# Low parts of the last three units on one engine, and own tiles for the last residual rows

## The chip, the core and the metric

The kernel runs on one core of a Trainium2 chip. The metric is the time of one execution on the device in microseconds (us). TensorE (PE) multiplies matrices, VectorE (DVE), ScalarE (ACT) and GpSimd (POOL) work elementwise, SyncE (SP) issues most of the transfers (DMA). Each engine runs its own instructions in program order, and they wait for each other through semaphores.

## What is computed

A block of two parts on `x` of 2 x 2048 rows of 512 numbers. With `ln` for a normalisation of rows:

```python
x = x + tanh(g_xattn) * xattn(ln(x), ctx, mask)   # 16 heads of 32, 128 keys for each batch
x = x + tanh(g_ffn) * ffn(ln(x))                  # residual inside: h + 0.5 * (silu(LN(h) @ w1 + b1) @ w2 + b2)
# xattn: q = LN(x) @ w_q; k, v = LN(ctx) @ w_kv; softmax(q k^T * scale + mask) v @ w_proj + b_proj
# w1 (512 x 2048), w2 (2048 x 512): (integers - 128) * scales
```

## The kernel before

**Precision.** Most products are made from split operands: a tile is kept as a high part and a low part (what the rounding left over), and `split_product` adds three matmuls (high*high, high*low, low*high; lines 219 to 221). So each operand costs an elementwise subtraction for its low part somewhere.

**Attention** (`attention`, the first 437 us). The 4096 rows are 8 chunks of 512 rows; a chunk is 4 units, each with one group of 4 heads (`HG`), so there are 32 units (`UNITS`), 0 to 31. Every engine walks through steps: step k works on unit k and, beside it, on neighbours: the queries of unit k+2, the maxima of unit k+1, the softmax of unit k, the weighted values of unit k-1, the projection of the row tile k-5, the residual sum of tile k-6. A row tile is 128 rows; 4 of them belong to a chunk. The first and the last steps are written out, the ones between run in a hardware loop; the order in each engine is the order in its `step` function.

**Probabilities.** For each of the four heads j, PE makes the scores into a bank `ps_s` (L522), ACT writes `p_f` (f32, L686) and `p_hi` (f16, L688) from it, and the low part `p_lo = p_f - p_hi` is made by DVE for j = 0 and 1 (L833) and by POOL for j = 2 and 3 (L1006). `weighted_values` (L537, then L541 for the sums of the probabilities) needs all eight parts and runs one step later, behind the maxima matmuls (L504) of the unit after. Its 28 matmuls run in groups of four, one for each head, so 12 + 8 + 8 of them stand in the rows. On DVE a step is: two maxima (L796), the residual sum `x_out = projection + x_res` (L841), two maxima, the inversion of the sums, `p_lo` 0 and 1, `normalise` (L825, `o_f`). The third maxima matmul waits for the first maximum (its bank), the fourth for the second.

**Residual rows.** For tile t, SP loads 128 rows of `x` into `x_res[t % 2]` in step t+4 (L408). That load waits until the residual sums up to tile t-2 are made (L841), as that frees the buffer. POOL adds the bias in step t+5 (`bias_residual`, L983), DVE makes the sum in step t+6, SP stores it (L415). At the end PE projects tiles 28 and 29 in step 33 and 30 and 31 in step 35, by turns into two banks (`ps_xp` for even tiles, `ps_qm` for odd ones); the projection of 31 needs the bank of 29, so it waits for the sum of tile 29.

**The change-over.** The weights of the second part are loaded into memory that attention has given up: `load_w2` is issued by ACT in step 32 (two transfers of 1 MB) after waits on the counts of `p_lo`. DVE and ACT make the first parts of w1 in steps 33 and 35 (L171, L160, L175). Then all engines leave attention together and start `feed_forward`: PE with L219 on `ps_y`, whose sums (`ps_z`, L1228 to L1230) wait for parts of w2 from DVE (L177).

**Memory.** `xt_f`, two tiles of 2 KB a partition, hold a transposed block of normalised x for its splitting. Attention uses them last for job 35, whose low part POOL makes in step 29. `xt_hi` and `xt_lo` are four tiles of 8 KB a partition; small tiles (statistics, scales, maxima) lie behind them.

Of the kernel before, what the change touches and what calls it, by code (L numbers as in the profile page):

```python
# [27 lines left out]
F32R = mybir.dt.float32r  # L28
# [3 lines left out]
ALU = mybir.AluOpType  # L32
# [3 lines left out]
P = 128  # L36
HEAD = 32
HG = P // HEAD
# [11 lines left out]
def build(nc, x, ctx, mask, g_xattn, g_ffn, w_q, w_kv, w_proj, b_proj, g_x, b_x, g_kv, b_kv,  # L50
# [22 lines left out]
    with ExitStack() as whole:  # L73
        def sb(name, shape, dt, scope=whole):
            return scope.enter_context(nc.sbuf_tensor(name, shape, dt))
# [14 lines left out]

        x_in, x_norm = sb("x_in", [P, TT, D], F32), sb("x_norm", [P, TT, D], F32)
        xt_f = [sb(f"xt_f{n}", [P, CHUNK], F32) for n in range(2)]
        xt_hi = [sb(f"xt_hi{n}", [P, KB, CHUNK], F32R) for n in range(2)]
        xt_lo = [sb(f"xt_lo{n}", [P, KB, CHUNK], F32R) for n in range(2)]
        stats, mean_var = sb("x_stats", [P, TT, 6], F32), sb("x_mean_var", [P, TT, 2], F32)
        ln_a, ln_r1, ln_b, ln_c, ln_r2, ln_s2, ln_r, u_scale = (
            sb(n, [P, TT], F32) for n in ("ln_a", "ln_r1", "ln_b", "ln_c", "ln_r2", "ln_s2", "ln_r", "u_scale"))
# [1 line left out]
        fill_col = sb("fill_col", [P, B], F32)  # L99
        ones16 = sb("ones16", [P, HEAD], BF16)  # L100
        maxima = [sb(f"maxima{n}", [P, TT, HG], F32) for n in range(2)]

# [120 lines left out]
def attention(nc, env):  # L225
# [30 lines left out]
    with ExitStack() as scope:  # L256
# [68 lines left out]
             "setup_over"))  # L325
        x_loaded = sem("x_loaded")
        res_loaded = [sem("res_loaded0"), sem("res_loaded1")]
        q_stored, q_packed, max_packed = ([sem(f"{name}{n}") for n in range(2)] for name in ("q_stored", "q_packed", "max_packed"))
        (stats_some, stats_ready, ln_step, rstd_ready, norm_ready, xt_turned, xt_f_ready, xt_hi_ready, xt_lo_ready,
         q_done, q_hi_ready, q_lo_ready, max_done, max_taken, max_turned, max_row_ready, s_done,  # L330
# [33 lines left out]
        def load_vectors(eng, which):  # L364
            for n in which:
                v, at = vectors[n], n * KB
                eng.dma_start(vec_rows[at:at + v.shape[0] // P, :], v.rearrange("(n p) -> n p", p=P)).then_inc(vec_loaded, 16)

        def proj_bank(i, k):

            return ps_qm if not real(i, k + KB, UNITS) and k % 2 else ps_xp
# [7 lines left out]
        def _(sp):  # L379
# [12 lines left out]
            def step(i, k):  # L392
                if real(i, k + 1, UNITS):
                    pack_queries(i, k + 1)
                if k == FIRST:
                    load_x(i, 0)
                if k % KB == 2:
                    load_x(i, k // KB + 3)
                tile = k - 4
                if isinstance(i, int) and PER * i + tile == 0:  # L400
                    sp.wait_ge(wq_lo_ready, 2)
                    sp.wait_ge(wp_lo_ready, 2)
                if real(i, tile, UNITS):
                    c, t = tile // KB, tile % KB
                    source = x_tiles[c % 2, i + c // 2, t, :, :]
                    sp.lower_val(source.offset * 4)
                    after(sp, x1_ready, PER * i + tile - 1)
                    sp.dma_start(x_res[t % 2][:, :], source).then_inc(res_loaded[t % 2], 16)  # L408
                tile = k - 6
                if real(i, tile, UNITS):  # L410
                    c, t = tile // KB, tile % KB
                    target = x1_tiles[c % 2, i + c // 2, t, :, :]
                    sp.lower_val(target.offset * 4)
                    after(sp, x1_ready, PER * i + tile + 1)
                    sp.dma_start(target, x1_out[t % 2][:, :]).then_inc(x1_stored[t % 2], 16)  # L415
                if real(i, k + 2, UNITS):
                    store_queries(i, k + 2)
                if real(i, k + 1, UNITS):
                    pack_maxima(i, k + 1)
# [62 lines left out]
        def _(pe):  # L482
# [42 lines left out]
            def weighted_values(i, k):  # L525


                v, b, m = PER * i + k, (k // KB) % 2, k % KB
                after(pe, p_hi_ready, HG * (v + 1))
                after(pe, p_lo_dve, HG // 2 * (v + 1))  # L530
                after(pe, p_lo_pool, HG // 2 * (v + 1))
                after(pe, o_f_ready, v)
                terms = [(v_parts[0], p_hi), (v_parts[1], p_hi), (v_parts[2], p_hi), (v_parts[0], p_lo), (v_parts[1], p_lo)]
                for n, (part, probs) in enumerate(terms):
                    for j in range(HG):
                        h = HG * m + j
                        nc.tensor.matmul(ps_o[HEAD * j:HEAD * (j + 1), :], part[:, b, h * HEAD:(h + 1) * HEAD], probs[j][:, :],  # L537
                                         start=(n == 0), stop=(n == len(terms) - 1))
                for n, probs in enumerate((p_hi, p_lo)):
                    for j in range(HG):  # L540
                        last = nc.tensor.matmul(ps_den[HEAD * j:HEAD * (j + 1), :], ones16[:, :], probs[j][:, :],  # L541
                                                start=(n == 0), stop=(n == 1))
                last.then_inc(pv_done, 1)
# [126 lines left out]
        def _(act):  # L670
# [6 lines left out]
            def probabilities(i, k, j):  # L677

                v, b = PER * i + k, (k // KB) % 2
                if isinstance(i, int) and v == 0 and j == 0:  # L680
                    act.wait_ge(fill_ready, 1)
                    act.wait_ge(setup_over, 2)
                after(act, s_done, HG * v + j + 1)

                after(act, p_lo_dve if j < HG // 2 else p_lo_pool, HG // 2 * (v - 1) + j % (HG // 2) + 1)
                nc.scalar.activation(p_f[j][:, :], ps_s[j % 2][:, :], ACT.Exp, bias=fill_col[:, b:b + 1]).then_inc(p_f_ready, 1)  # L686
                after(act, pv_done, v)
                nc.scalar.activation(p_hi[j][:, :], ps_s[j % 2][:, :], ACT.Exp, bias=fill_col[:, b:b + 1]).then_inc(p_hi_ready, 1)  # L688
# [84 lines left out]
            def last_steps(u):  # L773

                if u == UNITS - 2:
                    act.wait_ge(q_done, UNITS)
                    g("load_w1")(act, 0)
                if u == UNITS:
                    act.wait_ge(s_done, HG * UNITS)
                    act.wait_ge(p_lo_dve, HG // 2 * UNITS)  # L780
                    act.wait_ge(p_lo_pool, HG // 2 * UNITS)
                    g("load_w2")(act, 0)
                if u in (UNITS + 1, UNITS + 3):
                    g("weights_hi")(act, 0, (u - UNITS) // 2)
# [5 lines left out]
        def _(dve):  # L790
# [44 lines left out]
            def add_residual(i, k):  # L835
                tile = PER * i + k
                after(dve, proj_done, tile + 1)
                after(dve, res_biased, tile + 1)
                if real(i, k - 2, UNITS):
                    after(dve, x1_stored[k % 2], 8 * (tile - k % 2))  # L840
                nc.vector.tensor_tensor(x1_out[k % 2][:, :], proj_bank(i, k)[:, :], x_res[k % 2][:, :], ALU.add).then_inc(x1_ready, 1)  # L841

            def row_stats(i, c):
                if not real(i, KB * c, UNITS + KB):
# [23 lines left out]
            def step(i, k):  # L868
                if real(i, k + 1, UNITS):
                    take_max(i, k + 1, (0, 1))  # L870
                if real(i, k - 6, UNITS):
                    add_residual(i, k - 6)
                if real(i, k + 1, UNITS):
                    take_max(i, k + 1, (2, 3))
                if real(i, k + 2, UNITS):
                    queries_lo(i, k + 2)
                if k % KB == 0 and k != -KB:
                    row_stats(i, k // KB + 2)
                if k % KB == 1:
                    normalise_rows(i, k // KB + 2)  # L880
                if real(i, k - 1, UNITS):
                    invert_sums(i, k - 1)
                if real(i, k, UNITS):
                    probabilities_lo(i, k, 0)
                    probabilities_lo(i, k, 1)
                if real(i, k - 1, UNITS):
                    normalise(i, k - 1)
                if isinstance(i, int):
                    last_steps(PER * i + k)

# [88 lines left out]
        def _(pool):  # L979
            def bias_residual(i, k):  # L980
                tile = PER * i + k
                after(pool, res_loaded[k % 2], 8 * (tile - k % 2) + 16)
                nc.gpsimd.tensor_tensor(x_res[k % 2][:, :], x_res[k % 2][:, :], bp_rows[:, :], ALU.add).then_inc(res_biased, 1)  # L983

            def outputs_lo(i, k):
                v, c, m = PER * i + k, (k // KB) % 2, k % KB
# [48 lines left out]
            def step(i, k):  # L1035
                if real(i, k + AHEAD, UNITS + KB):
                    x_lo(i, k + AHEAD)
                if real(i, k - 5, UNITS):
                    bias_residual(i, k - 5)
                if k % KB == 0 and k != -KB:  # L1040
                    row_scales(i, k // KB + 2)
                if real(i, k, UNITS):
                    probabilities_lo(i, k, 2)
                    probabilities_lo(i, k, 3)
                if real(i, k - 1, UNITS):
                    outputs_lo(i, k - 1)
# [363 lines left out]
```

## Time and profile before

| what | us |
|---|---|
| median of 3 runs | 1169.83 |
| lowest and highest of them | 1168.03, 1169.94 |
| the profiled execution | 1169.56 |
| its span in the profile | 1167.7 |
| PE busy | 1102.7 |
| DVE, ACT, POOL busy | 631.1, 389.9, 343.0 |

The span runs from the first to the last instruction of the profile; the execution's own time is 1.86 us longer. "Idle before" in square brackets is how long the engine stood still before an instruction, and after the arrow who released it. `x4` behind a row says that four instructions are merged in it. `ps_z<-w_hi,y_hi` reads "writes ps_z, reads w_hi and y_hi"; buffer numbers are left out.

### The profile page before, as it was taken

How to read it: one execution, taken by the hardware profiler on the slowest of the kernel's cores; microseconds unless marked ns; L12 is line 12 of the kernel's file. 1: busy time of each engine (PE TensorE's matmuls, PEld its weight loads, DVE VectorE, ACT ScalarE, POOL GpSimd, SP SyncE). 2: the span in 40 equal slices, each digit the busy share in tenths (PEclk: the TensorE clock that was granted, in tenths of full speed). 3: DMA queues.
4: the chain of work that ended last, by engine and by line, in shares of the span. 5: the costliest groups of instructions: out<-in, count | busy, mean ns of one | idle time of the engine just before them, and what ended most of it. 6: DMA issues, size and time to landing. Idle time of an engine off the chain costs nothing.

```text
span 1167.7 us, 15594 instructions
## 1 busy us (share of the span) xinstructions
PE 1102.7 (94%) x5433; PEld 845.6 (72%) x5433; DVE 631.1 (54%) x1039; ACT 389.9 (33%) x614; POOL 343.0 (29%) x344
## 2 busy tenths in 40 slices
PE   5778999999989878999999999999999999999998
PEld 3455667666666547888888888888888888888887
DVE  5667788787796647765334335335235235235212
ACT  3467667667667623331121121121111111111110
POOL 4545576676675542202101102102102102012000
PEclk9879999999999989999999999999999999999999
DMA  7665666666655659501002001001000100200000
GB/s 257 154 190 139 180 190 189 203 181 186 210 154 164 186 175 314 155 1 73 1 1 72 1 1 48 25 1 39 33 0 30 42 0 1 72 1 1 37 1 36
DMA packets 61178, 109.20 MB, mean 94 GB/s; under 512 B 9368, under 2 KB 10560, under 8 KB 60608
## 3 DMA queue, kind: packets, MB, share of 16 engines
q1 hardware_dynamic: 58632, 104.11, 29.2%
q10 hardware_dynamic: 2488, 4.34, 1.2%
q8 instruction: 34, 0.56, 0.2%
q14 instruction: 24, 0.20, 0.1%
HBM read 72.51 MB, written 33.55 MB: 91 GB/s over the span
## 4 chain that ended last, share of the span: by engine, by line
PE 61%; DVE 1%; issue 0%; ACT 0%; DVEq 0%
PE ps_y L221 10%; PE ps_y L220 10%; PE ps_z L1228 10%; PE ps_z L1230 10%; PE ps_z L1229 10%; PE ps_y L219 10%; PE ps_h L1242 1%; DVE x_in L1348 0%; DVE x L1311 0%; DVE y_hi L1288 0%; DVE w_lo L177 0%; DVE w_f L171 0%; ACT w_hi L162 0%; DVE y_lo L1290 0%; DVEq L47 0%
## 5 line engine op out<-in xcount | busy, mean ns | idle before, releaser
L1288 DVE CAST y_hi<-y_f 128x512 fp32r<-128x512 f32 x128 | 63.3, 494 | 391.5 <-ACT y_f L1263 391.5
L1263 ACT ACTIVATE y_f<-ps_y,cols 128x512 f32<-128x512 f32 x128 | 88.1, 689 | 552.7 <-PE ps_y L221 552.7
L1228 PE MATMUL ps_z<-w_hi,y_hi 128*128 128x512 f32 x512 | 203.1, 397 | 3.0 <-DVE w_lo L177 3.0
L219 PE MATMUL ps_y<-xt_hi,w_hi 128*128 128x512 f32 x512 | 202.1, 395 | 1.5 <-PEq L256 1.5
L221 PE MATMUL ps_y<-xt_hi,w_lo 128*128 128x512 f32 x512 | 203.4, 397 | 0.0
L220 PE MATMUL ps_y<-xt_lo,w_hi 128*128 128x512 f32 x512 | 202.9, 396 | 0.0
L1230 PE MATMUL ps_z<-w_hi,y_lo 128*128 128x512 f32 x512 | 200.8, 392 | 0.0
L1229 PE MATMUL ps_z<-w_lo,y_hi 128*128 128x512 f32 x512 | 200.4, 391 | 0.0
L219 PEld LDWEIGHTS ps_y<-xt_hi,w_hi 128*128 128x128 f32 x512 | 96.3, 188 | 24.7 <-issue 1.9
L1228 PEld LDWEIGHTS ps_z<-w_hi,y_hi 128*128 128x128 f32 x512 | 96.5, 188 | 23.8 <-DVE w_lo L177 3.4
L220 PEld LDWEIGHTS ps_y<-xt_lo,w_hi 128*128 128x128 f32 x512 | 96.7, 189 | 22.8
L221 PEld LDWEIGHTS ps_y<-xt_hi,w_lo 128*128 128x128 f32 x512 | 96.2, 188 | 22.5
L1230 PEld LDWEIGHTS ps_z<-w_hi,y_lo 128*128 128x128 f32 x512 | 96.4, 188 | 21.1
L1229 PEld LDWEIGHTS ps_z<-w_lo,y_hi 128*128 128x128 f32 x512 | 96.6, 189 | 20.8
L1290 DVE TENSOR_TENSOR y_lo<-y_f,y_hi 128x512 fp32r<-128x512 f32 x128 | 96.4, 753 | 4.4
L1006 POOL TENSOR_TENSOR p_lo<-p_f,p_hi 128x512 f16<-128x512 f32 x64 | 78.9, 1243 | 63.9 <-ACT p_hi L688 63.5
L796 DVE TENSOR_REDUCE maxima<-ps_max 128x4 f32<-128x512 f32 x128 | 81.9, 680 | 13.4 <-PE ps_max L504 13.2
L686 ACT ACTIVATE p_f<-ps_s,fill_col 128x512 f32<-128x512 f32 x128 | 86.3, 674 | 5.1 <-PE ps_s L522 5.1
L688 ACT ACTIVATE p_hi<-ps_s,fill_col 128x512 f16<-128x512 f32 x128 | 85.4, 667 | 0.0
L1366 POOL TENSOR_TENSOR ln_a<-x_mean_var,eps 128x4 f32<-128x4 f32 x7 | 1.5, 216 | 273.0 <-DVE x_mean_var L1333 273.0
L997 POOL TENSOR_TENSOR xt_lo<-xt_f,xt_hi 128x512 fp32r<-128x512 f32 x36 | 46.7, 1300 | 85.6 <-ACT xt_f L698 82.8
L1384 POOL TENSOR_TENSOR x<-x,b_rows 128x512 f32<-128x512 f32 x16 | 26.3, 1672 | 153.3 <-DVE x L1348 153.3
(161 smaller groups left out, 1615.3 us busy)
## 6 DMA issues: line engine op xcount, KB each, us to landing
q_pack<-q_dram SPq DMA_DIRECT2D x96, 256.0 KB, 3.9
x_in<-in_x SPq DMA_DIRECT2D x8, 1024.0 KB, 7.5
q_dram<-q_hi SPq DMA_DIRECT2D x32, 256.0 KB, 2.9
q_dram<-q_lo SPq DMA_DIRECT2D x32, 256.0 KB, 3.3
x_res<-in_x SPq DMA_DIRECT2D x32, 256.0 KB, 3.9
x_dram<-x_out SPq DMA_DIRECT2D x32, 256.0 KB, 4.2
q_raw<-in_L_ffn_fc_q SPq DMA_DIRECT2D x6, 1024.0 KB, 18.6
s_raw<-in_L_ffn_fc_scales SPq DMA_DIRECT2D x6, 1024.0 KB, 17.1
```

The source lines that it names most:

```text
L219: nc.tensor.matmul(out, s_hi, m_hi, start=(k == 0), stop=False)
L220: nc.tensor.matmul(out, s_hi, m_lo, start=False, stop=False)
L221: last = nc.tensor.matmul(out, s_lo, m_hi, start=False, stop=(k == n - 1))
L686: nc.scalar.activation(p_f[j][:, :], ps_s[j % 2][:, :], ACT.Exp, bias=fill_col[:, b:b + 1]).then_inc(p_f_ready, 1)
L688: nc.scalar.activation(p_hi[j][:, :], ps_s[j % 2][:, :], ACT.Exp, bias=fill_col[:, b:b + 1]).then_inc(p_hi_ready, 1)
L796: nc.vector.reduce_max(maxima[k % 2][:, t, :], ps_max[t % 2][:, :].rearrange("p (j n) -> p j n", j=HG), AX.X).then_inc(max_taken, 1)
L1006: nc.gpsimd.tensor_tensor(p_lo[j][:, :], p_f[j][:, :], p_hi[j][:, :], ALU.subtract).then_inc(p_lo_pool, 1)
L1228: nc.tensor.matmul(ps_z[t][:, :], hi, w2_hi[:, f, :], start=(f == 0), stop=False)
L1229: nc.tensor.matmul(ps_z[t][:, :], hi, w2_lo[:, f, :], start=False, stop=False)
L1230: last = nc.tensor.matmul(ps_z[t][:, :], lo, w2_hi[:, f, :], start=False, stop=(f == FB - 1))
L1263: nc.scalar.activation(y_f[f % 2][:, :], ps_y[f % 2][:, :], ACT.Silu, bias=b1_c[:, f:f + 1]).then_inc(y_f_ready, 1)
L1290: nc.vector.tensor_tensor(y_lo[f % 4][:, :], y_f[f % 2][:, :], y_hi[f % 4][:, :].bitcast(F32), ALU.subtract).then_inc(y_lo_ready, 1)
```

## The change

Three things. In units 29, 30 and 31 DVE makes the low parts of heads 2 and 3 too, after `normalise` and ahead of the next step; POOL makes none there. The counts that PE and ACT wait for are adapted (`lo_counts`, `lo_taken`). The residual rows of tiles 30 and 31 go into `xt_f[0]` and `xt_f[1]`; SP loads both in step 30, once the low part of job 35 is made, in place of the loads in steps 34 and 35. And `xt_hi`, `xt_lo` are allocated behind the small tiles, which so move down by four times 8 KB.

```diff
@@ build
-        xt_hi = [sb(f"xt_hi{n}", [P, KB, CHUNK], F32R) for n in range(2)]
-        xt_lo = [sb(f"xt_lo{n}", [P, KB, CHUNK], F32R) for n in range(2)]
         stats, mean_var = sb("x_stats", [P, TT, 6], F32), sb("x_mean_var", [P, TT, 2], F32)
...
         maxima = [sb(f"maxima{n}", [P, TT, HG], F32) for n in range(2)]
+        xt_hi = [sb(f"xt_hi{n}", [P, KB, CHUNK], F32R) for n in range(2)]
+        xt_lo = [sb(f"xt_lo{n}", [P, KB, CHUNK], F32R) for n in range(2)]
@@ attention
+        last_res_loaded = [sem(f"last_res_loaded{n}") for n in range(2)]
+        def in_tail(i, k):
+            return isinstance(i, int) and PER * i + k >= UNITS - 3
+        def lo_counts(i, k):
+            v = PER * i + k
+            more = max(0, v + 1 - (UNITS - 3)) if isinstance(i, int) else 0
+            return HG // 2 * (v + 1 + more), HG // 2 * (v + 1 - more)
+        def lo_taken(i, k, j):
+            v = PER * i + k
+            if in_tail(i, k):
+                return p_lo_dve, lo_counts(i, k - 1)[0] + j + 1
+            return p_lo_dve if j < HG // 2 else p_lo_pool, HG // 2 * v + j % (HG // 2) + 1
+        def last_pair(i, k):
+            return isinstance(i, int) and PER * i + k >= UNITS - 2
+        def residual(i, k):
+            return xt_f[k % 2][:, :] if last_pair(i, k) else x_res[k % 2][:, :]
@@ SP, step
-                if real(i, tile, UNITS):
+                if real(i, k, UNITS) and PER * i + k == UNITS - 2:
+                    sp.wait_ge(xt_lo_ready, UNITS + KB)
+                    for n in range(2):
+                        sp.dma_start(xt_f[n][:, :], x_tiles[(NCHUNK - 1) % 2, (NCHUNK - 1) // 2, KB - 2 + n, :, :]
+                                     ).then_inc(last_res_loaded[n], 16)
+                if real(i, tile, UNITS) and not last_pair(i, tile):
@@ PE, weighted_values
-                after(pe, p_lo_dve, HG // 2 * (v + 1))
-                after(pe, p_lo_pool, HG // 2 * (v + 1))
+                after(pe, p_lo_dve, lo_counts(i, k)[0])
+                after(pe, p_lo_pool, lo_counts(i, k)[1])
@@ ACT, probabilities
-                after(act, p_lo_dve if j < HG // 2 else p_lo_pool, HG // 2 * (v - 1) + j % (HG // 2) + 1)
+                after(act, *lo_taken(i, k - 1, j))
@@ ACT, last_steps
-                    act.wait_ge(p_lo_dve, HG // 2 * UNITS)
-                    act.wait_ge(p_lo_pool, HG // 2 * UNITS)
+                    act.wait_ge(p_lo_dve, lo_counts(0, UNITS - 1)[0])
+                    act.wait_ge(p_lo_pool, lo_counts(0, UNITS - 1)[1])
@@ DVE, add_residual
-                nc.vector.tensor_tensor(x1_out[k % 2][:, :], proj_bank(i, k)[:, :], x_res[k % 2][:, :], ALU.add).then_inc(x1_ready, 1)
+                nc.vector.tensor_tensor(x1_out[k % 2][:, :], proj_bank(i, k)[:, :], residual(i, k), ALU.add).then_inc(x1_ready, 1)
@@ DVE, step
                 if real(i, k - 1, UNITS):
                     normalise(i, k - 1)
+                if real(i, k, UNITS) and in_tail(i, k):
+                    probabilities_lo(i, k, 2)
+                    probabilities_lo(i, k, 3)
@@ POOL, bias_residual
-                after(pool, res_loaded[k % 2], 8 * (tile - k % 2) + 16)
-                nc.gpsimd.tensor_tensor(x_res[k % 2][:, :], x_res[k % 2][:, :], bp_rows[:, :], ALU.add).then_inc(res_biased, 1)
+                if last_pair(i, k):
+                    pool.wait_ge(last_res_loaded[k % 2], 16)
+                else:
+                    after(pool, res_loaded[k % 2], 8 * (tile - k % 2) + 16)
+                nc.gpsimd.tensor_tensor(residual(i, k), residual(i, k), bp_rows[:, :], ALU.add).then_inc(res_biased, 1)
@@ POOL, step
-                if real(i, k, UNITS):
+                if real(i, k, UNITS) and not in_tail(i, k):
                     probabilities_lo(i, k, 2)
                     probabilities_lo(i, k, 3)
```

## Rows read from the trace of the kernel before

**Rows 1.** The page: span and the first line of part 1.
```profile
span 1167.7 us, 15594 instructions
...
PE 1102.7 (94%) x5433; PEld 845.6 (72%) x5433; DVE 631.1 (54%) x1039; ACT 389.9 (33%) x614; POOL 343.0 (29%) x344
```

**Rows 2.** Windows: busy PE, PEld, DVE, ACT, POOL, then clock, DMA share, GB/s.
```profile
300.00:400.00 100.00, 93.14 (x597) 63.17 (x595) 77.45 (x125) 68.01 (x116) 60.62 (x54) 0.98 0.60 172
400.00:420.00 20.00, 13.91 (x86) 7.90 (x87) 8.48 (x14) 7.10 (x13) 10.43 (x10) 0.83 0.55 164
420.00:440.00 20.00, 15.34 (x60) 11.88 (x59) 10.81 (x11) 3.58 (x4) 8.83 (x7) 0.91 0.68 228
```

**Rows 3.** Waits of PE, 380 to 470 us: us in total, times, longest.
```profile
PE ps_o L537 <- POOL p_lo L1006: 6.4, 3, 2.9
PE ps_qm L219 <- DVE x_out L841: 3.1, 1, 3.1
...
PE ps_z L1228 <- DVE w_lo L177: 3.0, 1, 3.0
```

**Rows 4.** Timeline at unit 29: start, duration, instruction, idle before.
```profile
389.47 0.69 DVE L833 TENSOR_TENSOR p_lo<-p_f,p_hi 128x512 f16<-128x512 f32 x1 [0.45 <-ACT p_hi L688]
...
390.08 0.68 DVE L825 TENSOR_TENSOR o_f<-ps_o,inv_den 128x512 f32<-128x512 f32 x1
...
390.66 2.35 POOL L1006 TENSOR_TENSOR p_lo<-p_f,p_hi 128x512 f16<-128x512 f32 x2 [2.18 <-ACT p_hi L688]
390.74 1.29 DVE L796 TENSOR_REDUCE maxima<-ps_max 128x4 f32<-128x512 f32 x2
391.03 0.68 ACT L688 ACTIVATE p_hi<-ps_s,fill_col 128x512 f16<-128x512 f32 x1
...
391.58 1.01 PE L504 MATMUL ps_max<-k_hi,q_hi 128*128 128x512 f32 x2 [0.72 <-DVE maxima L796]
...
391.95 0.68 DVE L841 TENSOR_TENSOR x_out<-ps_xp,x_res 128x512 f32<-128x512 f32 x1
...
393.26 0.83 PE L537 MATMUL ps_o<-p_hi,v 128*32 128x512 f16 x12 [0.67 <-POOL p_lo L1006]
```

**Rows 5.** Timeline at units 30 and 31.
```profile
399.67 2.34 POOL L1006 TENSOR_TENSOR p_lo<-p_f,p_hi 128x512 f16<-128x512 f32 x2 [4.20 <-ACT p_hi L688]
...
400.04 0.68 ACT L688 ACTIVATE p_hi<-ps_s,fill_col 128x512 f16<-128x512 f32 x1
...
402.26 1.47 PE L537 MATMUL ps_o<-p_hi,v 128*32 128x512 f16 x12 [2.85 <-POOL p_lo L1006]
...
412.23 1.46 PE L537 MATMUL ps_o<-p_hi,v 128*32 128x512 f16 x12 [2.85 <-POOL p_lo L1006]
```

**Rows 6.** Timeline of PE: two waits of 1.7 us in earlier units.
```profile
215.11 1.09 PE L504 MATMUL ps_max<-k_hi,q_hi 128*128 128x512 f32 x2 [1.73 <-DVE maxima L796]
...
349.10 1.00 PE L504 MATMUL ps_max<-k_hi,q_hi 128*128 128x512 f32 x2 [1.70 <-DVE maxima L796]
...
350.86 0.63 PE L220 MATMUL ps_qm<-xt_lo,wq_hi 128*128 128x512 f32 x1
```

**Rows 7.** Timeline of the last tiles.
```profile
418.54 0.69 DVE L841 TENSOR_TENSOR x_out<-ps_xp,x_res 128x512 f32<-128x512 f32 x1 [0.52 <-PE ps_xp L221]
...
419.26 0.33 SPq L408 DMA_DIRECT2D x_res<-in_x  x1
...
427.42 2.48 POOL L983 TENSOR_TENSOR x_res<-x_res,bp_rows 128x512 f32<-128x512 f32 x2 [5.16 <-DMA x_res<-in_x]
...
428.77 0.69 DVE L841 TENSOR_TENSOR x_out<-ps_qm,x_res 128x512 f32<-128x512 f32 x1 [4.20 <-POOL x_res L983]
...
435.52 0.69 DVE L841 TENSOR_TENSOR x_out<-ps_qm,x_res 128x512 f32<-128x512 f32 x1 [0.67 <-PE ps_qm L221]
...
437.02 0.47 PE L219 MATMUL ps_y<-xt_hi,w_hi 128*128 128x512 f32 x1 [1.54 <-PEq L256]
```

**Rows 8.** The bias sums, ns: least, median, most.
```profile
L983 POOL TENSOR_TENSOR x_res<-x_res,bp_rows x7: 1262/1270/2278, 394.2 to 432.5; 128x512 f32<-128x512 f32 x7
```

## The prediction

> **What bounds the kernel now.** I read the page first: PE is busy for 94% of the span, so a change elsewhere counts only where PE stands still or its clock is down [rows 1]. The windows show where that is near the change. From 300 to 400 us PE is busy for 93% at a granted clock of 0.98; from 400 to 420 us for 70% at 0.83, from 420 to 440 us for 77% at 0.91 [rows 2]. The list of waits says on what: 6.4 us in three waits for the low parts on POOL, 3.1 us once for a residual sum, 3.0 us once for a part of w2, which comes behind the change-over [rows 3]. The first is what the moved low parts aim at, the second is where the residual tiles would have to act. The timelines say what is behind each.
>
> **The low parts, units 30 and 31.** In unit 30 ACT finishes the last `p_hi` at 400.04 + 0.68 = 400.72, POOL has both low parts at 399.67 + 2.34 = 402.01, and PE starts at 402.26, 0.25 later [rows 5]. On DVE the third low part can be made while ACT works on the fourth head. The fourth starts when `p_hi` is there, plus the hand-over from engine to engine: the first of the two bias sums ends at 427.42 + 1.24 = 428.66 and DVE starts at 428.77, so 0.11 [rows 7]. It takes 0.69 [rows 4]. That is 400.72 + 0.11 + 0.69 = 401.52, against 402.01: 0.5 us earlier. Unit 31 has the same wait of 2.85 [rows 5], so 0.5 us again. Nothing that PE wants soon stands behind them on DVE there: there are no more maxima, and the residual sum that moves behind them feeds a projection that PE reaches after its weighted values. Gain 1.0 us; bounds: 0, if the hand-over to PE is longer from DVE, and 1.2.
>
> **The low parts, unit 29.** Here the maxima of unit 31 stand behind them. Before, DVE goes from `o_f` at 390.08 straight into two maxima at 390.74 (1.29, so 0.645 each), and PE's third maxima matmul starts 0.2 after the first of them, at 391.58 [rows 4]. Now DVE waits for the last `p_hi` (391.03 + 0.68 = 391.71), has the fourth low part at 391.71 + 0.11 + 0.69 = 392.51 and the first maximum at 393.15. PE's third maxima matmul starts at 393.35 and, with the pair's 1.01 kept, the weighted values at about 394.2 to 394.4, where they start at 393.26 now [rows 4]. So this unit loses 0.9 to 1.1 us, of which the wait of 0.67 for POOL is already taken off. I take 1.0. It is on PE's path: the turned maxima come behind the weighted values in PE's order, and the second pair of maxima is late by as much. Queued on DVE behind the same wait are the residual sum of tile 24 (0.68) and two more maxima; that sum delays two transfers on SP, which has a step of room for them.
>
> **The sum of the low parts** is +1.0 - 0.5 - 0.5 = 0.0 us. ACT loses nothing: its waits on the low parts are for those of the unit before.
>
> **The residual tiles.** PE's 3.1 us is the projection of tile 31, which waits for the sum of tile 29 (428.77). That sum waits 4.20 for the bias sum, and this one 5.16 for its load [rows 7]. That is the load of tile 29, issued at 419.26, as soon as the sum of tile 27 (418.54) has freed the buffer [rows 7]. Tile 29 is not one of the two that get tiles of their own, and its buffer is still freed by tile 27. So PE's wait stays. What changes is behind it: the loads of 30 and 31 are early, and the bias sum of 31 follows that of 30 at once. But the sum of tile 31 waits 0.67 for PE, not for its residual [rows 7]. Gain 0; lower bound 0, upper bound 3.1, if the load of 29 came early by other means. SP issues two transfers (0.33 each, by the same kind [rows 7]) in step 30 in place of two later ones. Its new wait is for work of step 29, so it is over; behind it are a load, a store and the packing of the maxima of unit 31, wanted a step later. Cost 0, and 0.7 if that room were not there.
>
> **POOL beside DVE.** The bias sums take 1.27 in the median and 2.28 in one case [rows 8], so a neighbour can hold one up. With the bias sum of 31 moved forward it falls on DVE's second part of w1. If DVE stands still for it, that is 1.27, of which the wait of 0.67 covers half [rows 7]; the other 0.6 is the upper bound. I take 0, as the sum of tile 30 between them waits for its projection as well. The Trainium skill ("SBUF — State Buffer", the section on SBUF's two separate sides) has it that VectorE with two SBUF inputs and GpSimd reading SBUF exclude each other for a whole instruction. It speaks against putting more two-input work on DVE beside POOL, and by it the full 1.27 would be paid on DVE; the longest row above fits it.
>
> **The memory.** Small tiles and `xt_hi`, `xt_lo` change addresses and no instruction changes shape. No row shows a duration that depends on an address. Cost 0; bounds 0.3 either way, the agreement that rows of one kind show (1262 and 1270 ns, the least and the median [rows 8], so under 1% of what touches the tiles).
>
> **The clock.** The 12 matmuls behind the waits of 2.85 take 1.47 and those at 393.26 take 0.83 [rows 4, 5]: the clock is at 1.2 instead of 2.4 GHz there. For 28 matmuls that is 28/12 x 0.64 = 1.5 us, the price of one fall. The waits of 2.85 become 2.35, and a new idle stretch appears in step 30: from 390.86 (391.58 less the 0.72 idle) to 393.35, 2.5 us, where the clock does not fall now. Is 2.35 or 2.5 enough? A stretch of 1.73 at 215 us was not; one of 1.70 at 349 us was, the matmul at 350.86 takes 0.63 [rows 6]; both of 2.85 were. So more likely than not for each of the three, and not certain for any. The likeliest number of falls stays at two. [...]
>
> **Forecast.** 0.0 us from low parts, residuals and memory, with two falls as before. The profiled execution took 1169.56 (span 1167.7), 0.3 below the median of the runs. The forecast of no change goes onto the median: 1169.8. Chance 0.45.
>
> **Rival 1: a third fall** in step 30, none saved: +1.5, 1171.3. For it: the new stretch of 2.5 us. Against it: the 1.73 at 215 us. Chance 0.27. It is slower, but under the bound below.
>
> **Rival 2: the shorter waits save the clock** in one or both of units 30 and 31: -1.5, 1168.3, or -3.0, 1166.8. Chance 0.14, of that 0.04 for both.
>
> **Rival 3: tile 29 is helped after all**, as its load no longer shares the queues with later ones: the 3.1 us go, and the fall of the clock behind them: up to -4.6, 1165.2. Against it: at 419.26 the loads of 30 and 31 were not issued yet. Chance 0.05.
>
> **Rival 4: slower.** The place is the maxima of unit 31 on DVE. The loss of 1.0 is there and the clock falls (1.5); it decides if the low parts of units 30 and 31 give back nothing, because PE's start there is then set by the delayed chain of maxima, their packing and the scores: +2.5, 1172.3. Against it: packing has a step of room. Chance 0.07. That addresses matter, or that the change does not do what it says, has 0.02.
>
> **Range and chances.** A measurement can tell 0.2%, 2.3 us, from no change. The forecast, rival 1 and single savings lie inside. Faster: both savings (0.04), rival 3 (0.05) and the scatter of the runs, which reach 1.8 below their median (0.03): 0.12. Slower: rival 4 (0.07) and the scatter on top of rival 1 with half of the rest (0.04): 0.11. Same: 0.77. The range from 1167.6 to 1171.8 holds the forecast, rival 1 and rival 2 with one saving.
>
> **What would show it.** In the profile after: weighted values of unit 29 about 1 us later (start near 394.3), those of 30 near 402.8, of 31 near 412.2, each behind DVE's low parts instead of POOL's; an idle stretch of 2.5 us before the maxima matmul; the wait of about 3 us for the sum of tile 29 unchanged, with the load of 29 landing some 8 us after its issue; PE's start on `ps_y` within 0.5 us of 437.0 but for the clock, whose share from 390 to 420 us tells the number of falls. I am wrong if that start is over 2.3 us away, or if the wait for the sum of tile 29 is gone.

## The result and the profile after

| | kernel before | changed kernel |
|---|---|---|
| median of 3 runs, us | 1169.83 | 1152.72 |
| lowest and highest, us | 1168.03, 1169.94 | 1151.14, 1154.12 |
| ratio, 95% interval | | 0.9858 [0.9833, 0.9883] |
| span of the profiled execution, us | 1167.7 | 1150.9 |

The changed kernel is 17 us faster. I had forecast no change, 1167.6 to 1171.8 us. Measured once more, beside 11 runs of the kernel before, it gained 12.5 us (changed_again below), so a few of the 17 us are scatter of the runs. The page of the changed kernel, the lines that answer to [rows 1]:

```profile
span 1150.9 us, 15594 instructions
...
PE 1082.7 (94%) x5433; PEld 841.0 (73%) x5433; DVE 634.4 (55%) x1045; ACT 390.1 (34%) x614; POOL 337.1 (29%) x338
```

PE is busy for 20 us less with the same 5433 matmuls, and its share of the span is still 94%. It did not wait less; its matmuls got shorter. Six elementwise instructions went from POOL to DVE, as the diff says.

**Where the time went.** I cut the span at two marks that both timelines have. The first is the `normalise` of unit 28, the last DVE instruction ahead of the new low parts; the second is PE's first matmul on `ps_y`, the start of the second part. The timeline of the changed kernel, DVE and then PE, has

```profile
386.28 0.68 DVE L856 TENSOR_TENSOR o_f<-ps_o,inv_den 128x512 f32<-128x512 f32 x1
...
432.83 0.47 PE L219 MATMUL ps_y<-xt_hi,w_hi 128*128 128x512 f32 x1 [1.54 <-PEq L256]
```

and the kernel before has these marks at 390.08 and 437.02 [rows 4, 7].

| stretch | before, us | after, us | difference |
|---|---|---|---|
| start to the first mark | 390.08 | 386.28 | -3.8 |
| first to second mark (low parts, residual tiles) | 46.94 | 46.55 | -0.4 |
| second mark to the end | 730.7 | 718.1 | -12.6 |

The stretch that I had worked through row by row moved by 0.4 us. Three quarters of the gain is in the second part, in which no instruction was changed. The groups of PE from 700 to 1000 us show it, first for the kernel before (count | busy us, mean ns | idle):

```profile
L1228 PE MATMUL ps_z<-w_hi,y_hi 128*128 128x512 f32 x214 | 84.7, 396 | 0.0
L221 PE MATMUL ps_y<-xt_hi,w_lo 128*128 128x512 f32 x212 | 84.2, 397 | 0.0
L220 PE MATMUL ps_y<-xt_lo,w_hi 128*128 128x512 f32 x212 | 84.0, 396 | 0.0
L219 PE MATMUL ps_y<-xt_hi,w_hi 128*128 128x512 f32 x212 | 83.6, 394 | 0.0
L1229 PE MATMUL ps_z<-w_lo,y_hi 128*128 128x512 f32 x214 | 83.5, 390 | 0.0
```

and for the changed one:

```profile
L1265 PE MATMUL ps_z<-w_hi,y_hi 128*128 128x512 f32 x216 | 85.2, 394 | 0.0
L221 PE MATMUL ps_y<-xt_hi,w_lo 128*128 128x512 f32 x218 | 84.8, 389 | 0.0
L219 PE MATMUL ps_y<-xt_hi,w_hi 128*128 128x512 f32 x217 | 84.4, 389 | 0.0
L220 PE MATMUL ps_y<-xt_lo,w_hi 128*128 128x512 f32 x217 | 84.4, 389 | 0.0
L1267 PE MATMUL ps_z<-w_hi,y_lo 128*128 128x512 f32 x216 | 84.1, 390 | 0.0
```

In the same 300 us, 212 matmuls of each line on `ps_y` became 217 or 218. The matmuls are back to back, without idle time, at full clock. All have one shape. Yet before, those that write `ps_y` took 394 to 397 ns and one that writes `ps_z` 390; after, those on `ps_y` took 389. The `ps_z` row with `w_hi,y_hi` fits neither: it is the longest on `ps_z` before (396) and after (394). As durations overlap, start to start is the better measure. Medians by position in the group of twelve that a step makes, worked out from the start times behind 500 us (a sum is good to 3 ns, as some medians waver between 226 and 227):

```
ps_y before   234 232 231 232 238 237 231 234 235 233 232 237   sum 2806 ns
ps_y after    227 227 227 227 226 227 227 227 227 227 227 227   sum 2723 ns
ps_z before   231 232 231 227 226 227 227 227 227 227 227 227   sum 2736 ns
ps_z after    227 226 227 227 227 227 227 226 227 227 226 227   sum 2721 ns
```

That is 98 ns a step, and 128 steps make 12.5 us, nearly all of the second part's gain. The first three matmuls on `ps_z` were slow before too (231, 232, 231), though neither of their tiles moved; they stand right behind the matmuls on `ps_y`. How the pace reaches over to them is not shown. `ps_y` reads `xt_hi` and `xt_lo` as moving tiles, the ones whose place in memory the change moves; the weights stay where they were.

**Before the second part.** The queries of attention read the same tiles, in 384 matmuls. Start to start on `ps_qm` they take 233 ns before and 227 after in the median, 233.7 and 229.1 in the mean, so they make 1.8 to 2.3 us of the 3.8. The rest fits the clock, granted at 0.84 from 60 to 100 us before and at 0.91 after, and at 0.66 from 350 to 355 us before and at 1.00 after. The first window of the changed kernel, then the second of the kernel before:

```profile
60.00:100.00 40.00, 30.20 (x187) 18.73 (x186) 27.97 (x50) 28.54 (x49) 18.27 (x20) 0.91 0.60 173
```

```profile
350.00:355.00 5.00, 5.00 (x39) 2.73 (x37) 2.03 (x4) 2.04 (x3) 1.02 (x2) 0.66 0.51 179
```

**The stretch of the forecast.** The windows that answer to [rows 2]:

```profile
400.00:420.00 20.00, 16.68 (x105) 11.59 (x106) 13.05 (x19) 7.13 (x11) 8.50 (x6) 0.91 0.75 236
420.00:440.00 20.00, 15.28 (x60) 11.92 (x59) 12.17 (x12) 3.22 (x4) 11.04 (x7) 0.91 0.53 188
```

PE's waits from 376 to 466 us, against [rows 3]:

```profile
PE ps_z L1265 <- DVE w_lo L177: 3.2, 1, 3.2
PE ps_qm L219 <- DVE x_out L872: 3.2, 1, 3.2
PE ps_max L535 <- DVE maxima L827: 2.4, 1, 2.4
PE ps_o L568 <- ACT p_hi L719: 2.2, 1, 2.2
PE ps_o L568 <- DVE p_lo L864: 2.2, 1, 2.2
```

The wait for the sum of tile 29 is still there (3.2), the two of 2.85 became 2.20, and a new one of 2.39 is in front of the maxima matmul. The timeline of PE, against [rows 4, 5]:

```profile
389.46 1.00 PE L535 MATMUL ps_max<-k_hi,q_hi 128*128 128x512 f32 x2 [2.39 <-DVE maxima L827]
390.39 0.83 PE L568 MATMUL ps_o<-p_hi,v 128*32 128x512 f16 x12
391.05 0.96 PE L568 MATMUL ps_o<-p_lo,v 128*32 128x512 f16 x8
...
393.46 1.20 PE L553 MATMUL ps_s<-q_pack,k_pack 97*128 97x512 f32 x2
...
400.14 0.83 PE L568 MATMUL ps_o<-p_hi,v 128*32 128x512 f16 x12 [2.20 <-DVE p_lo L864]
...
402.06 1.22 PE L553 MATMUL ps_s<-q_pack,k_pack 97*128 97x512 f32 x2
...
409.50 0.83 PE L568 MATMUL ps_o<-p_hi,v 128*32 128x512 f16 x12 [2.20 <-ACT p_hi L719]
```

From the first mark to the weighted values of unit 29 it is 390.39 - 386.28 = 4.11 us, and 3.18 before: 0.93 later. From 391 us on the clock is down (eight matmuls in 0.96, two score matmuls in 1.20). The clock fell behind the new gap, as rival 1 had it. The clock fell again after the start of unit 30's values, and was up for unit 31's.

And the last tiles, DVE and POOL, against [rows 7]:

```profile
423.10 1.26 POOL L1020 TENSOR_TENSOR x_res<-x_res,bp_rows 128x512 f32<-128x512 f32 x1 [5.04 <-DMA x_res<-in_x]
424.32 3.50 POOL L1020 TENSOR_TENSOR xt_f<-xt_f,bp_rows 128x512 f32<-128x512 f32 x2
...
424.45 0.69 DVE L872 TENSOR_TENSOR x_out<-ps_qm,x_res 128x512 f32<-128x512 f32 x1 [4.24 <-POOL x_res L1020]
425.06 1.61 DVE L171 SCALAR_TENSOR_TENSOR w_f<-q_raw,s_raw 128x1024 f32<-128x1024 int32 x1
```

The bias sum of tile 29 still waits for its load (issued at 414.94), while those of 30 and 31 follow at once. Nothing of PE waited for these.

### The profile page after: what moved, and what is told of

It is laid out like the page before. It is cut to its first block, busy times and chain, and to the rows that moved or that the text cites. A ratio compares the mean times of both kernels' runs of the same rounds, so it can differ in the third digit from the quotient of the medians.

```text
span 1150.9 us, 15594 instructions
## 1 busy us (share of the span) xinstructions
PE 1082.7 (94%) x5433; PEld 841.0 (73%) x5433; DVE 634.4 (55%) x1045; ACT 390.1 (34%) x614; POOL 337.1 (29%) x338
## 4 chain that ended last, share of the span: by engine, by line
PE 61%; DVE 1%; issue 0%; ACT 0%; DVEq 0%
PE ps_z L1265 10%; PE ps_z L1267 10%; PE ps_z L1266 10%; PE ps_y L219 10%; PE ps_y L220 10%; PE ps_y L221 10%; PE ps_h L1279 1%; DVE x_in L1385 0%; DVE x L1348 0%; DVE y_hi L1325 0%; DVE w_lo L177 0%; DVE w_f L171 0%; ACT w_hi L162 0%; DVE y_lo L1327 0%; DVEq L47 0%
## 5 line engine op out<-in xcount | busy, mean ns | idle before, releaser
L219 PE MATMUL ps_y<-xt_hi,w_hi 128*128 128x512 f32 x512 | 199.5, 390 | 1.5 <-PEq L256 1.5
L221 PE MATMUL ps_y<-xt_hi,w_lo 128*128 128x512 f32 x512 | 199.3, 389 | 0.0
L220 PE MATMUL ps_y<-xt_lo,w_hi 128*128 128x512 f32 x512 | 199.2, 389 | 0.0
L1043 POOL TENSOR_TENSOR p_lo<-p_f,p_hi 128x512 f16<-128x512 f32 x58 | 71.8, 1248 | 51.3 <-ACT p_hi L719 51.0
```

The costliest lines, as they stand in the source:

```text
L219: nc.tensor.matmul(out, s_hi, m_hi, start=(k == 0), stop=False)
L220: nc.tensor.matmul(out, s_hi, m_lo, start=False, stop=False)
L221: last = nc.tensor.matmul(out, s_lo, m_hi, start=False, stop=(k == n - 1))
L1043: nc.gpsimd.tensor_tensor(p_lo[j][:, :], p_f[j][:, :], p_hi[j][:, :], ALU.subtract).then_inc(p_lo_pool, 1)
```

## The experiments

All times of "the kernel before" below are of the same chip and job. Its median was 1166.9 to 1167.9 us there. Addresses are those that the build gives, in bytes within a partition.

### Which part of the change

Theory A: the place of the split x tiles relative to the weights. Theory B: the other two parts.

**mem_only** is the kernel before with only this:

```diff
-        xt_hi = [sb(f"xt_hi{n}", [P, KB, CHUNK], F32R) for n in range(2)]
-        xt_lo = [sb(f"xt_lo{n}", [P, KB, CHUNK], F32R) for n in range(2)]
...
         maxima = [sb(f"maxima{n}", [P, TT, HG], F32) for n in range(2)]
+        xt_hi = [sb(f"xt_hi{n}", [P, KB, CHUNK], F32R) for n in range(2)]
+        xt_lo = [sb(f"xt_lo{n}", [P, KB, CHUNK], F32R) for n in range(2)]
```

> Kernel before with one part of the change: xt_hi and xt_lo allocated behind the small tiles, nothing else. Theory A (the place of the split x tiles relative to the weights sets the pace of the matmuls that read both): nearly all of the gain, 15 to 17 us under the kernel before, about 1153.5 us, and start to start of the matmuls on ps_y 227 ns instead of 233 to 235. Theory B (the gain comes from the low parts and the residual tiles, and the faster matmuls are a matter of this chip or run): no change, about 1170 us, 233 ns or more.

Measured: 1155.88 us, ratio 0.989 [0.9857, 0.9924]; `ps_y` at 227 ns. **no_mem** is the changed kernel with the same lines put back.

> Changed kernel with xt_hi and xt_lo back in front of the small tiles; low parts and residual tiles as changed. Theory A: as the kernel before within 0.2 percent, 1168 to 1171 us (the blind sum of these two parts was 0.0), matmuls on ps_y at 233 ns or more. Theory B: about 1153 us.

Measured: 1168.7 us, ratio 1.0006 [0.9985, 1.0026]; `ps_y` at 231 to 238 ns by position, 233.8 in the mean. The two together settle it. The order of memory alone makes a gain of 11 us, and the other two parts without it make none. B falls. The gain of mem_only was smaller than the 15 to 17 us expected; repeated below it was 14.

### What about the place

In the kernel before `xt_hi` begins at 24576 and the weights at 57952; in the changed one at 25184 and 57952. **x0_w0** puts 32 unused bytes behind the small tiles.

```diff
         maxima = [sb(f"maxima{n}", [P, TT, HG], F32) for n in range(2)]
+        sb("pad_w", [P, 8], F32)
```

> Kernel before with 32 unused bytes a partition behind the small tiles. xt_hi stays at an address that 64 divides (24576); the weights of both parts and all later tiles move from 32 past such an address to one that 64 divides (57984). Theory A1 (what costs is that the moving tile and the weights stand 32 bytes apart modulo 64): as fast as the changed kernel, about 1153 us, all matmuls at 227 ns. Theory A2 (what costs is the moving tile's own address dividing by 64): slow as before, 1170 us, or slower, as the moving tiles of ps_z and of the projection are then on such addresses too (up to 10 us more).

**x32_w0** puts them in front of `xt_hi`.

```diff
+        sb("pad_x", [P, 8], F32)
         xt_hi = [sb(f"xt_hi{n}", [P, KB, CHUNK], F32R) for n in range(2)]
```

> Kernel before with 32 unused bytes a partition in front of xt_hi, so that it stands 32 past a multiple of 64 (24608) and the weights on one (57984). Theory A1: slow as before, about 1170 us, ps_y at 233 ns or more. Theory A2: ps_y fast at 227 ns; the matmuls whose moving tile is now on a multiple of 64 (ps_z) slow, in sum about as the kernel before, so the pace by line decides between A1 and A2, not the time.

Measured: 1165.27 us, ratio 0.9969 [0.9944, 0.9995], and 1166.4 us, ratio 0.9993 [0.9975, 1.0012]. Neither became fast: x0_w0 speaks against A1, x32_w0 against A2. The paces told more than the times:

```
ps_y, x0_w0    234 224 238 229 237 229 237 229 238 229 237 229   sum 2790 ns
ps_y, x32_w0   234 232 231 232 238 237 231 234 235 233 232 237   sum 2806 ns
```

x32_w0 has, position by position, the numbers of the kernel before. Both tiles are 32 bytes further there, their distance is the same. x0_w0 has another distance and another pattern. So I formed A3: it is the distance of the moving tile from the weights, modulo something. As the pattern is the same for each of the four column blocks of w1, which lie 512 bytes apart, the distance counts modulo 512 at most. Against it stood A4: all kernels without the gain had `xt_hi` at 0 or 32 modulo 2048.

**x0_w0_d0** leaves `xt_hi` where it is and moves the weights to distance 0:

```diff
         maxima = [sb(f"maxima{n}", [P, TT, HG], F32) for n in range(2)]
+        sb("pad_w", [P, 360], F32)
```

> Kernel before, order of memory kept, with 1440 unused bytes a partition behind the small tiles: xt_hi stays at 24576 (a multiple of 2048), the weights and all later tiles go to a multiple of 2048 as well (59392). Distance modulo 2048 zero as in the changed kernel, but at another place. Theory A3 (the pace of a matmul depends on the distance between its moving tile and the weights that are loaded beside it, modulo 256 or 512 bytes: 0 is fast, 96 and 128 are slow): fast, 12 to 17 us under the kernel before, ps_y at 227 ns, with no part of the memory order of the change. Theory A4 (the moving tile's own place is what counts, 0 and 32 modulo 2048 are slow, 608 and 640 fast): slow, 1167 us or more (about 10 us more, as the moving tile of ps_z is then there too).

Measured: 1154.38 us, ratio 0.988 [0.984, 0.9919], `ps_y` and `ps_z` at 227 ns everywhere. One line of padding gives what the change gave. A4 falls.

**y_off96** makes the damage in another place. On `ps_z` the roles are turned: w2 is the moving tile and y is loaded as weights. It is the changed kernel with

```diff
+            fb("pad_y", [P, 24], F32)
             y_f = [fb(f"y_f{n}", [P, CHUNK], F32) for n in range(2)]
```

> Changed kernel with 96 unused bytes a partition in front of the y tiles, so that the loaded weights of ps_z (y_hi, y_lo) stand 96 bytes from their moving tile (w2) modulo 512, the distance that ps_y has in the kernel before. Nothing else moves but the y tiles. Theory A3: the slow pace changes over from ps_y to ps_z: ps_y at 227 ns, the twelve ps_z matmuls of a step about 80 ns longer in sum, 10 to 13 us over the changed kernel in 128 steps, about 1165 us. Theory A4: no change from the changed kernel, 1153 us.

Measured: 1165.21 us, against 1152.7 for the changed kernel in its own job; ratio to the kernel before 0.9978 [0.9957, 0.9999]. The groups of PE from 700 to 1000 us (columns as above):

```profile
L1266 PE MATMUL ps_z<-w_hi,y_hi 128*128 128x512 f32 x214 | 86.0, 402 | 0.0
L1268 PE MATMUL ps_z<-w_hi,y_lo 128*128 128x512 f32 x214 | 84.7, 396 | 0.0
L1267 PE MATMUL ps_z<-w_lo,y_hi 128*128 128x512 f32 x214 | 84.5, 395 | 0.0
L220 PE MATMUL ps_y<-xt_hi,w_hi 128*128 128x512 f32 x212 | 82.9, 391 | 0.0
L221 PE MATMUL ps_y<-xt_lo,w_hi 128*128 128x512 f32 x212 | 82.9, 391 | 0.0
```

The slow pace has changed sides: `ps_z` now has 395 to 402 ns and `ps_y` 391. The twelve on `ps_z` have the pattern that `ps_y` had, shifted:

```
ps_z, y_off96  231 232 237 237 231 234 235 233 232 237 237 231   sum 2807 ns
```

To see after how many bytes the pattern repeats, **d64** and **d256** are mem_only with 64 and 256 unused bytes between `xt_lo` and the weights (here d64; d256 has 64 in place of 16):

```diff
         xt_lo = [sb(f"xt_lo{n}", [P, KB, CHUNK], F32R) for n in range(2)]
+        sb("pad_w", [P, 16], F32)
```

> Kernel before with the memory order of the change and 64 unused bytes between xt_lo and the later tiles: distance 64 modulo 512, xt_hi at 608 modulo 2048. Theory A3: slow, 230 to 236 ns on ps_y, 1162 to 1170 us. Theory A4: fast, 1153 us.

> The same with 256 unused bytes. Theory A3: if the pattern repeats after 256 bytes, as fast as with 0 (227 ns, 1153 us); if only after 512, slow (230 ns or more). Theory A4: fast.

Measured: 1163.42 us, ratio 0.9958 [0.9938, 0.9978], each `ps_y` matmul at 233 ns; and 1152.89 us, ratio 0.9867 [0.9811, 0.9923], each at 227. The windows of d64, then of d256, from 900 to 1000 us:

```profile
900.00:1000.00 100.00, 100.00 (x443) 81.24 (x442) 37.16 (x64) 14.36 (x21) 11.23 (x13) 1.00 0.10 35
```

```profile
900.00:1000.00 100.00, 100.00 (x450) 82.82 (x450) 38.08 (x66) 15.11 (x23) 11.40 (x13) 1.00 0.08 28
```

443 matmuls against 450 in 100 us at full clock. Together, with the time from the second mark to the end in each profile:

| kernel | distance of the weights from xt modulo 256 | twelve ps_y, ns | second mark to the end, us |
|---|---|---|---|
| changed, mem_only, x0_w0_d0 | 0 | 2720 to 2724 | 718.1, 718.2, 720.1 |
| d256 | 0 (256 modulo 512) | 2724 | 718.1 |
| d64 | 64 | 2796 | 731.6 |
| before, no_mem, x32_w0 | 96 | 2806 | 730.7, 731.9, 730.1 |
| x0_w0 | 128 | 2790 | 729.8 |

y_off96, with distance 0 on `ps_y` and 96 on `ps_z`, has 731.5 us there.

### What the other two parts add

**mem_again**, **lo_only** and **changed_again** ran together, with **all_zero**. lo_only is the changed kernel with

```diff
         def last_pair(i, k):
-            return isinstance(i, int) and PER * i + k >= UNITS - 2
+            return False
...
-                if real(i, k, UNITS) and PER * i + k == UNITS - 2:
+                if False:
```

> Kernel before with only the memory order of the change, once more, beside the other three of this job: base for what the other two parts add. About 1155 us.

> Memory order and the low parts on VectorE, residual rows of tiles 30 and 31 as before. My blind sum for the low parts (+1.0 for unit 29, -0.5 for each of 30 and 31) gives the memory order alone, give or take one fall of the clock (1.5 us): 1153.5 to 1156.5 us. Rival (the shorter waits spare the clock in units 30 and 31): 1.5 to 3 us under the memory order alone.

> The changed kernel itself, once more. If the residual tiles gain nothing, as forecast, it is as the kernel with memory order and low parts within 1 us; if they gain the 3.1 us of PE's wait for the sum of tile 29, 3 us less.

> Low parts and residual tiles of the change, memory order of before, and 1440 unused bytes in front of the weights, so that x_norm, the split x tiles, the weights and all later tiles stand at multiples of 256 bytes. Theory A3 says as fast as the changed kernel; and if x_norm (read for the transposes beside the split tiles) counts as well, up to 1 us under it.

| kernel | median, us | ratio to the kernel before |
|---|---|---|
| mem_again | 1152.75 | 0.9884 [0.9861, 0.9908] |
| lo_only | 1152.95 | 0.988 [0.9859, 0.99] |
| changed_again | 1154.4 | 0.989 [0.987, 0.9909] |
| all_zero | 1152.74 | 0.9885 [0.9867, 0.9903] |

The four can't be told apart. The low parts add nothing that can be measured to the memory order, and the residual tiles nothing on top of them. The changed kernel itself gains 12.5 us here. all_zero is no_mem with the padding of x0_w0_d0, so `x_norm`, the split tiles, the weights and all later tiles are at multiples of 256; it gains nothing over the changed kernel. No version here beats it beyond the intervals.

## Why the prediction was wrong

**The step that failed is "The memory".** It said "Cost 0; bounds 0.3 either way". The step measured -11 us in mem_only, -14 when repeated. What the runs showed in its place: with the split x tiles 96 bytes from the weights modulo 256, each matmul that reads both takes 7 ns more from start to start than at distance 0, and the whole kernel is 11 to 14 us longer. Three things were wrong in the step. "No row shows a duration that depends on an address" rested on rows of other engines: I had read the waits and the change-over, but not the matmuls of one shape against each other. The page of the kernel before had them:

```profile
L1228 PE MATMUL ps_z<-w_hi,y_hi 128*128 128x512 f32 x512 | 203.1, 397 | 3.0 <-DVE w_lo L177 3.0
L219 PE MATMUL ps_y<-xt_hi,w_hi 128*128 128x512 f32 x512 | 202.1, 395 | 1.5 <-PEq L256 1.5
L221 PE MATMUL ps_y<-xt_hi,w_lo 128*128 128x512 f32 x512 | 203.4, 397 | 0.0
L220 PE MATMUL ps_y<-xt_lo,w_hi 128*128 128x512 f32 x512 | 202.9, 396 | 0.0
L1230 PE MATMUL ps_z<-w_hi,y_lo 128*128 128x512 f32 x512 | 200.8, 392 | 0.0
L1229 PE MATMUL ps_z<-w_lo,y_hi 128*128 128x512 f32 x512 | 200.4, 391 | 0.0
```

One shape and next to no idle time, and 3 to 6 ns between the three on `ps_y` and the last two on `ps_z`. The first row on `ps_z` breaks the pattern with 397, and does so in the changed kernel too (395). So these rows were a reason to look, and no proof. Then the bound was taken from POOL's bias sums, an engine that does other work, and put onto PE. And it was not multiplied out: `xt_hi` and `xt_lo` are read by 1536 + 384 matmuls on an engine that is busy for 94% of the span. The 8 ns in 1262 that I named are 0.6%, and 0.6% of 1920 matmuls at 234 ns are 2.8 us, not 0.3; the 6 ns of these rows are 11.5 us. With 11.5 as the bound the range would have begun at 1158.3 us, and the measured 1152.72 would still lie below it. Start to start, 7 ns each are 13.4 us.

The sign of being wrong that the prediction named did show: PE's start on `ps_y` is at 432.83, 4.2 us from 437.0. Of these, 3.8 come from the stretch ahead of the first mark.

**The low parts** came out as worked through. Unit 29 lost 0.93 us (forecast 1.0); the third maxima matmul came 389.46 - 386.28 = 3.18 after the first mark against 1.50 before, 1.68 later (1.77). The waits of 2.85 shrank by 0.65 each (0.5): in unit 30 DVE's last low part ends at 399.35 + 0.69 = 400.04 and PE starts at 400.14, 0.10 later, where it started 0.25 after POOL. For unit 31 the profile names ACT, but DVE's last low part ended there 0.10 before PE's start as well. lo_only against mem_again agrees with the sum of 0 within the scatter of the runs.

**The clock** went in this profile as rivals 1 and 2 described, at once: a third fall in step 30 and one spared in unit 31. So their prices cancelled, and the stretch moved by 0.4 us only; that is luck, and not the forecast of two falls as before. The other profiles show it. All six kernels with the moved low parts have the new gap of 2.38 or 2.39 us, and the clock fell at it in four (changed, changed_again, no_mem, all_zero) and not in two (lo_only, y_off96). Unit 31 was spared in two of the six. x0_w0, without the moved low parts, had a fall at this place as well (granted 0.64 from 390.5 to 394 us), with waits of 0.72 and 0.68 us only. With the fall in step 30 it fits that unit 30's values start 13.86 us after the first mark, where 12.7 was forecast. The gap in lo_only, then in no_mem:

```profile
391.14 1.01 PE L535 MATMUL ps_max<-k_hi,q_hi 128*128 128x512 f32 x2 [2.38 <-DVE maxima L827]
...
392.74 0.60 PE L568 MATMUL ps_o<-p_lo,v 128*32 128x512 f16 x8
```

```profile
390.55 1.30 PE L535 MATMUL ps_max<-k_hi,q_hi 128*128 128x512 f32 x2 [2.38 <-DVE maxima L827]
...
393.04 1.07 PE L568 MATMUL ps_o<-p_lo,v 128*32 128x512 f16 x8
```

mem_only and mem_again, the same kernel, differ in their first mark by as much as 2.5 us (388.40 and 385.94), so the stretch ahead of it is scatter to this size in any single profile.

**The residual tiles** gained nothing, as forecast, and for the reason given: 3.2 us for the sum of tile 29, whose bias sum starts 8.16 us after its load is issued (423.10 - 414.94), as before.

**POOL beside DVE**: the two bias sums of 30 and 31 took 3.50 us, the second of them 2.27, where the median is 1.27. It runs beside DVE's second part of w1 (L171, from 425.06), which had started 0.5 us before it and kept the 1.61 us that it took before. So POOL paid for the overlap here, and DVE, which the prediction's upper bound let pay, did not. In the kernel before the bias sum of 31 was lengthened too (1.96). It cost the end nothing.

**Rivals 3 and 4** did not come about. My 0.02 for an effect of addresses was far too little, and it was only listed for a loss.

## What to carry to other kernels

Compare instructions of one shape on the engine that bounds the kernel: if their mean differs by a few ns without idle time, ask which tiles they read and where these stand. A change of an allocation is a change to every instruction that reads the tile; multiply the smallest difference that the rows show by their number before calling it nothing. In this kernel, padding that puts moving tiles and weights a multiple of 256 bytes apart is worth 1.2% (x0_w0_d0), for one line.

## What the runs showed of the hardware

In a back-to-back stream of matmuls of 128x512 (fp32r), each with its own weights, one starts every 227 ns when the weights stand a multiple of 256 bytes from the moving tile within a partition, and every 232.5 to 234 ns in the mean at distances of 64, 96 and 128. For distance 96, x32_w0 and the kernel before have the same pattern over twelve matmuls at other addresses, and y_off96 has it shifted on other tiles; so it goes by the distance. The Trainium skill ("TensorE: Matmul & The Clock Gate", "Step-by-step: what each phase is for") says that loading the next tile's weights does not steal read bandwidth from the running matmul. The runs show that the pace does depend on where the two tiles stand relative to each other: the same matmuls and weight loads take 2.4 to 3% more at the other distances. That the two reads get in each other's way would explain it, and is not shown.

Behind an idle stretch of PE of 2.38 to 2.39 us the granted clock fell from 2.4 to 1.2 GHz in four profiles and stayed up in two.

Left open: whether it is the moving tile against its own weights or against those loaded while it runs, as here both have the same distance; why; distances other than these; and why the projections in attention, at distance 0 in all kernels, start every 231 ns in the median (231 to 233 over the kernels) while other engines are busy.
